# A mixture stage whose expert sum is split between VectorE, ScalarE and TensorE

## The reference

```python
logits = (h @ router_w.T + router_b).reshape(T, O, E)
probs = softmax(logits, axis=-1)
w, sel = top_k(probs, 2)
w = w / sum(w, axis=-1, keepdims=True)
c = zeros((T, E)).at[t_idx, sel].add(w)          # summed over all columns o
expert_out = einsum('th,eoh->teo', h, expert_w) + expert_b
final = einsum('te,teo->to', c, expert_out)
x = x + final
```

## Time and profile before

| | us |
|---|---|
| median of 3 runs (1189.95 to 1190.75) | 1190.35 |
| the profiled execution's own time | 1194.26 |
| its span | 1192.5 |
| mixture, first to last DVE instruction | 288.96 to 598.6 |
| busy in the span: PE / DVE / ACT / POOL | 1005.9 / 857.1 / 498.4 / 311.4 |
| busy from 288.9 to 598.7: PE / DVE / ACT / POOL | 239.26 / 291.58 / 165.23 / 113.89 |

### The profile page before, as it was taken

One profiled execution on the slowest core, in us unless ns is written; L12 is line 12 of the kernel. 1 busy time (PEld: TensorE's weight loads), 2 busy tenths in 40 slices (PEclk: granted clock), 3 DMA queues, 4 the chain that ended last, 5 costly groups with the idle time before them and its releaser, 6 DMA issues. The chain is left out here.

```text
span 1192.5 us, 19875 instructions
## 1 busy us (share of the span) xinstructions
PE 1005.9 (84%) x6885; PEld 588.9 (49%) x6960; DVE 857.1 (72%) x1556; ACT 498.4 (42%) x972; POOL 311.4 (26%) x337
## 2 busy tenths in 40 slices
PE   3698989888788798797487898898989799999997
PEld 1344545445444454353134474474657465556554
DVE  5677767643999899999967754746582776777766
ACT  2154444354464564646334313314230344444443
POOL 3243424531532524333320202203135400000000
PEclk9799989998899798898789898898897999999999
DMA  6622222101001000010000000001001000000000
GB/s 172 112 73 90 64 81 67 58 2 45 1 1 44 1 27 18 0 45 1 0 18 6 23 11 16 21 2 26 11 24 46 22 1 18 1 18 0 18 1 18
DMA packets 37088, 35.87 MB, mean 30 GB/s; under 512 B 8585, under 2 KB 33417, under 8 KB 37009
## 3 DMA queue, kind: packets, MB, share of 16 engines
q1 hardware_dynamic: 35728, 33.79, 9.8%
q10 hardware_dynamic: 1280, 1.05, 0.7%
HBM read 27.28 MB, written 6.29 MB: 28 GB/s over the span
## 5 line engine op out<-in xcount | busy, mean ns | idle before, releaser
L883 DVE TENSOR_REDUCE bm<-ps 128x4 f32<-128x512 f32 x160 | 102.1, 684 | 33.4 <-PE ps L603 31.7
L782 ACT ACTIVATE pt<-ps 128x1024 f32<-128x1024 f32 (+1 forms) x96 | 82.1, 882 | 72.5 <-PE ps L679 71.9
L1753 DVE TENSOR_TENSOR qk_lo<-ps,qk_hi 128x512 bf16<-128x512 f32 x80 | 54.9, 687 | 67.1 <-ACT qk_hi L1646 60.8
L2001 ACT ACTIVATE g<-ps 128x512 f32<-128x512 f32 x64 | 38.2, 597 | 134.1 <-PE ps L1948 107.4
L156 POOL TENSOR_TENSOR mag_w<-stage 128x512 f32<-128x512 fp8e4 x24 | 26.4, 1100 | 224.7 <-DVE stage L143 224.7
L2051 DVE SCALAR_TENSOR_TENSOR g<-g,ps 128x512 f32<-128x512 f32 x64 | 44.0, 688 | 54.5 <-ACT g L2001 54.2
L599 PE MATMUL ps<-ks,qs 96*128 96x512 bf16 (+3 forms) x256 | 66.7, 314 | 12.4 <-DMA ks<-scratch_k 7.7
L1646 ACT ACTIVATE qk_hi<-ps 128x512 bf16<-128x512 f32 x80 | 47.8, 599 | 69.4 <-PE ps L1515 69.4
L547 POOL TENSOR_SCALAR_AFFINE_SELECT pt<-pt 128x256 f32<-128x256 f32 (+1 forms) x96 | 47.2, 498 | 110.9 <-ACT pt L782 110.3
L1515 PE MATMUL ps<-wp_hi,oT_hi 128*128 128x256 bf16 x256 | 71.1, 278 | 5.0 <-DVE oT_lo L1746 5.0
L1964 PE MATMUL ps<-ew_hi,it_hi 128*128 128x256 bf16 x256 | 69.8, 273 | 6.1 <-DVE it_lo L2067 6.1
(11 more groups left out here) (272 smaller groups left out, 2840.9 us busy)
## 6 DMA issues: line engine op xcount, KB each, us to landing
qs<-scratch_q SPq DMA_DIRECT2D x64, 64.0 KB, 2.6
ks<-scratch_k SPq DMA_DIRECT2D x48, 64.0 KB, 2.6
q_next<-in_w_qkv SPq DMA_DIRECT2D x4, 768.0 KB, 4.4
X<-in_x SPq DMA_DIRECT2D x4, 512.0 KB, 7.0
w_next<-in_router_w SPq DMA_DIRECT2D x4, 512.0 KB, 3.7
w_next<-in_expert_w SPq DMA_DIRECT2D x4, 512.0 KB, 4.6
p_next<-in_w_proj SPq DMA_DIRECT2D x4, 512.0 KB, 5.4
out<-X SPq DMA_DIRECT2D x8, 256.0 KB, 2.3
```

The costliest lines, as they stand in the source:

```text
L782: act.activation(pt[kt][:, heads[0]:heads[-1] + 1, :], src, ACT.Exp).then_inc(s_exp, 1)
L883: ins = dve.tensor_reduce(bm[:, 2 * g + i // 5, 4 * (i % 5):4 * (i % 5) + 4], src.rearrange("p (k q) -> p k q", k=4), AX_X, ALU.max)
L1753: dve.tensor_tensor(qk_lo[:, k, h, :], bank(QK_BANK[m]), qk_hi[:, k, h, :], ALU.subtract).then_inc(s_qklo, 1)
```

## The change

`weigh` is cut in two. Experts 4 to 7 stay on DVE, as four multiply-adds. Experts 0 to 3 go to ACT, which writes psum * cw to a new tile `y` (`scaled_experts(n)`, behind `logits(n + 2)` and in front of `sigmoids(n + 1)`), and to PE, which sums the four parts of `y` with four fp32 matmuls against the identity into bank 4 (`scaled_sum(n - 1)`, behind `router(n + 2)`, or first in the iteration at t = 2). DVE adds that bank to X as its fifth instruction. PE fills the banks in the order 5, 6, 7, 4; bank 4 is free only when the whole `weigh(n - 1)` is done.

`two_greatest` is cut in two as well. Its first two instructions become `first_pairs`, done for tile n + 2. DVE's order in iteration n becomes: rest of `two_greatest(n + 1)`, `from_second(n + 1)`, statistics (t = 0), `first_pairs(n + 2)`, `masked(n + 1)`, `weigh(n)`. In the last two tiles the mask stays behind `weigh`. The tile `both` is gone; its place is taken by `n1`.

```diff
                 def experts(n, t):
-                    for u in range(NU):
-                        reach(pe, s_c, E * (n - 1) + 2 * (u + 1))
+                    for u in EXPERT_BANKS:                       # (1, 2, 3, 0)
+                        if u >= NY // 2:                         # NY = 4
+                            reach(pe, s_c, NX * (n - 1) + 2 * u + 2 - NY)   # NX = 5
+                        elif u == 0:
+                            reach(pe, s_c, NX * n)
+                def scaled_sum(n):
+                    pe.wait_ge(s_y, NY * n + NY)
+                    for e in range(NY):
+                        mm = pe.matmul(bank(4, D), ident[:, :], y[:, e, :], start=(e == 0), stop=(e == NY - 1),
+                                       skip_group_check=True)
+                    mm.then_inc(s_acc, 1)
                         if routed and t != 2:
                             router(routed[0], n + 2, routed[1])
+                        if not first or t:
+                            scaled_sum(n - 1)
                         experts(n, t)
+                def scaled_experts(n, t):
+                    act.wait_ge(s_cw, E * n + E)
+                    reach(act, s_acc, n)
+                    for u in EXPERT_BANKS:
+                        if u >= NY // 2:
+                            continue
+                        act.wait_ge(s_u, NU * n + EXPERT_BANKS.index(u) + 1)
+                        for e in (2 * u, 2 * u + 1):
+                            act.activation(y[:, e, :], bank(4 + u, D, D * (e % 2)), ACT.Copy,
+                                           scale=cw[t % 2][:, e:e + 1]).then_inc(s_y, 1)
+                        scaled_experts(n, t)
                         if after:
                             sigmoids(n + 1)
                 def weigh(b, n, t):
-                    for u in range(NU):
-                        dve.wait_ge(s_cw, E * n + 2 * u + 2)
-                        dve.wait_ge(s_u, NU * n + u + 1)
-                        for e in (0, 1):
-                            dve.scalar_tensor_tensor(x, bank(4 + u, D, D * e), c_t[:, 2 * u + e:2 * u + e + 1], x,
-                                                     ALU.mult, ALU.add).then_inc(s_c, 1)
-                            dve.wait_ge(s_c, E * n + 2 * u + e + 1)
+                    dve.wait_ge(s_cw, E * n + E)
+                    for i, e in enumerate(range(NY, E)):
+                        dve.wait_ge(s_u, NU * n + EXPERT_BANKS.index(e // 2) + 1)
+                        dve.scalar_tensor_tensor(x, bank(4 + e // 2, D, D * (e % 2)), c_t[:, e:e + 1], x,
+                                                 ALU.mult, ALU.add).then_inc(s_c, 1)
+                        dve.wait_ge(s_c, NX * n + i + 1)
+                    dve.wait_ge(s_acc, n + 1)
+                    dve.tensor_tensor(x, bank(4, D), x, ALU.add).then_inc(s_c, 1)
                         if after and not (first and t == 0):
-                            two_greatest(n + 1, after[1])
-                        weigh(b, n, t)
+                            two_greatest(n + 1)
+                        if after:
+                            from_second(n + 1, after[1])
                         if t == 0 and not last:
                             statistics(b + 1)
+                        if routed:
+                            first_pairs(n + 2, routed[1])
+                        if after and routed:
+                            masked(n + 1)
+                        weigh(b, n, t)
+                        if after and not routed:
+                            masked(n + 1)
                         if last and t == 1:
                             next_statistics()
-                        if after:
-                            from_second(n + 1, after[1])
-                            masked(n + 1)
```

More of the change, by code:

```diff
@@ L166 @@
 NU = EO // BANK
+NY = 4
+NX = E - NY + 1
+EXPERT_BANKS = (1, 2, 3, 0)
 STEP = 1.5 * 2.0 ** -22
@@ L969, in layer0_mixture @@
         h2, a2, c2 = (st.sb(n, [P, 2, D], F32) for n in ("h2", "a2", "c2"))
-        m1, n1, c1, m2, both, mid = (st.sb(n, [P, D], F32) for n in ("m1", "n1", "c1", "m2", "both", "mid"))
+        m1, n1, c1, m2, mid = (st.sb(n, [P, D], F32) for n in ("m1", "n1", "c1", "m2", "mid"))
         cw = [st.sb(f"cw{n}", [P, E], F32) for n in range(2)]
+        y = st.sb("y", [P, NY, D], F32)
         load_next, s_next, const = st.sem("load_next1"), st.sem("next1"), st.sem("const1")
@@ L982, in layer0_mixture @@
         s_abs, s_pert = st.sem("magnitudes"), st.sem("ties_broken")
+        s_y, s_acc = st.sem("experts_scaled"), st.sem("scaled_summed")
         stats2, mv2, rstd2 = (glob[n] for n in ("stats2", "mv2", "rstd2"))
@@ L1139, in _ @@
                 all_batches(pe, batch)
+                scaled_sum(4 * B - 1)
             @block.scalar
@@ L1258, in step, with first_pairs @@
                         dve.wait_ge(self.sem, self.start + self.done)
-                def two_greatest(n, t):
+                def first_pairs(n, t):
                     L = lg[t % 2]
@@ L1267, in two_greatest @@
                     do.step(dve.tensor_tensor(s4[:, :, :], L[:, 0:4, :], L[:, 4:8, :], ALU.min))
+                def two_greatest(n):
+                    do = Steps(s_top, TOP * n)
+                    do.done = 2
                     do.free(dve.tensor_tensor(h2[:, :, :], h4[:, 0:2, :], h4[:, 2:4, :], ALU.max))
@@ L1275, in two_greatest @@
                     do.step(dve.tensor_tensor(m2[:, :], n1[:, :], c1[:, :], ALU.max))
-                    do.step(dve.tensor_tensor(both[:, :], m1[:, :], m2[:, :], ALU.add))
+                    do.step(dve.tensor_tensor(n1[:, :], m1[:, :], m2[:, :], ALU.add))
                     if not isinstance(n, int) or n:
                         dve.wait_ge(s_mid, n)
-                    do.free(dve.tensor_scalar(mid[:, :], both[:, :], 0.5, None, ALU.mult))
+                    do.free(dve.tensor_scalar(mid[:, :], n1[:, :], 0.5, None, ALU.mult))
                     assert do.done == TOP
@@ L1311, in next_statistics @@
                 def next_statistics():
-                    dve.wait_ge(s_c, E * (4 * B - 3))
+                    dve.wait_ge(s_c, NX * (4 * B - 3))
                     for b in range(B):
@@ L1332, in next_low @@
                                           ALU.subtract)
-                two_greatest(0, 0)
+                first_pairs(0, 0)
+                two_greatest(0)
                 from_second(0, 0)
-                two_greatest(1, 1)
+                first_pairs(1, 1)
+                two_greatest(1)
                 masked(0)
                 def batch(b, first, last):
-                    for t, n, after, _ in tiles(b, last):
+                    for t, n, after, routed in tiles(b, last):
                         if t == 1 and not last:
```

## The result

The changed kernel takes **1230.17 us** (median of 4 runs, 1228.63 to 1232.07) against 1190.55 for the kernel before (4 runs, 1189.95 to 1192.47) on the same chip. The ratio is 1.0318, 95% interval 1.0290 to 1.0345: about 40 us slower. The forecast was 1218, its own range 1210 to 1232. The profiled execution took 1230.55, its span is 1228.8, 36.3 longer than before's. The two gaps differ because before's profiled execution (1194.26) lay 3.7 us above the median of its runs and after's only 0.4.

A forecast was written before the change was run, and what follows sets the result against it. The prediction took mutual exclusion between POOL's `wt` and DVE's two-SBUF-input instructions as the bound in every tile. Terms 1.6 + 5.5 + 14.4 + 7.5 - 1 gave +28.0 on 1190.35: 1218 us, own range 1210 to 1232, overall 1207 to 1234.

The forecast's parts named there:

- two batches of the loop: Mixture loop: tiles t = 0 to 3 lose 0.7, 0.9, 3.2 and 2.4 us, +7.2 a batch, +14.4 for two.
- tiles 13 to 15: Last batch: 61.4 us instead of 53.88, +7.5, with 19.1 each for tiles 13 and 14 and 23.2 for tile 15.
- The block (1): DVE between `mid` and mask: `far` and two comparisons exclude POOL's `wt`, together 8.99 us in every tile.
- The sums (2): DVE behind the mask: four sums plus a fifth instruction of 0.5, 2.9 us in the loop, 2.55 outside.
- ACT's lateness at t = 2 (3): Tile t = 2: late router, scalings and sigmoids end 0.4 to 1.8 us behind the comparisons; 0.8 taken, tile 21.1.
- The last root (5): Tile 15: POOL's root between statistics and `normalised` loses its cover and costs 1.7 us.
- The tail (6): Behind the last mask: the last sum ends 9.1 us after that mask's start instead of 10.3, so -1.
- PE's cost (7): PE in the mixture: 64 added fp32 matmuls, about 1.5 us a tile, cost zero; bounds 0 to +2 a batch.
- The range for unknowns: Whole change: ACT's lateness, fifth instruction, register waits, last root and PE's clock together give +20 to +42 us.
- no exclusion: First rival: `wt` runs beside `far` and comparisons, tile 17.25 us, 1192 us, no change; 6 in 100.
- DVE's count decides: Second rival: three fewer DVE instructions save 1.9 us a tile, 16 times, -30, so 1160 us; 5 in 100.
- PE becomes the bound: Rival: PE idles, its clock falls, tiles close through PE: +45 to +60, 1235 to 1250 us; 7 in 100.

The follow-up runs named there:

- e1: Kernel before with only DVE's order of the changed kernel, all eight sums staying on DVE behind the mask: 1248.26 us, ratio 1.0469.
- e2: Changed kernel with DVE's order of before, five sum instructions beside POOL's `wt`, scalings and scaled sum issued one step earlier: 1199.08 us, ratio 1.0058.
- e3: Changed kernel with `wt` made by DVE between `mid` and `far` instead of by POOL: 1202.89 us, ratio 1.0094.
- e5: Changed kernel with POOL's `wt` subtraction replaced by a memset of the same tile, so POOL only writes: 1172.34 us (one run).
- e10: e9 with one more move on PE: at t = 3 the scaled sum stands ahead of the router: 1218.54 us, ratio 1.0215.
- e9: Changed kernel; at t = 2 `x_low` ahead of the sums, router and ties ahead of the experts, scalings behind the sigmoids: 1229.48 us, ratio 1.0317.
- e6: e2 with four of `wt`'s eight experts made by DVE ahead of the sums, the rest by POOL beside them: 1186.19 us, ratio 0.9956.

## Why the prediction was right

The block of `far`, `wt` and two comparisons is within 0.6 us of the forecast in every tile but the three at t = 2, where ACT's late copies hide it, and the last, which has no comparisons. e1, e2, e3 and e5 each show it from another side. By the terms of the forecast, with what they measured from mask to mask:

| term | forecast | measured |
|---|---|---|
| tile 1 of batch 0 | +1.6 | +1.8 |
| tiles 2 to 4 | +5.5 | +7.0 |
| two batches of the loop | +14.4 | +17.0 |
| tiles 13 to 15 | +7.5 | +7.3 |
| tail | -1 | +1.3 |
| sum | +28.0 | +34.4 |

Another 1.25 us lie ahead of the first mask and 0.7 elsewhere in the span. Of the 11.8 us between the forecast and the median, 8.3 are in the span. The other 3.5 are the step from the span to the median: the forecast took off the 3.9 us by which before's profiled execution lay above its median, and after's lay only 0.4 above.

- **The block (1).** 8.99 us was the forecast for `far` and both comparisons; it is 8.95 in the last tile of batch 0 (382.75 to 391.70) and 8.96 in the loop (467.41 to 476.37). Right. At t = 1 it is 9.38, since POOL's small instruction stretches the second comparison (1.69 for 1.21).
- **The sums (2).** The fifth instruction was a bound between 0 and 0.52; it takes 0.42, in all 16 tiles, and four sums and addition take 2.4 us outside the loop and 2.5 in it, against 2.55 and 2.9. This, and not the block, makes t = 0 (18.9 for 19.45) and t = 3 (21.85 for 22.25) a little shorter. That t = 1 takes just the forecast 20.75 is luck: 0.4 less in the sums, 0.4 more in the block.
- **ACT's lateness at t = 2 (3).** The mis-sized term. "It starts 1.5 to 3 us behind `x_low`" was said of the router; it starts 4.6 behind (437.33 to 441.91). I had counted PE's work behind the sums at the full clock, 2.4 GHz; a lower one stood only among the unknowns. PE idles 5.6 us first, and its next 13 matmuls stand 0.43 us apart where they stand 0.215 apart at the full clock: 2.8 us. The trace of before could have told me: there too PE comes back at 0.50 after 5.19 us without work (window of the matmuls behind it):

```profile
464.60:469.00 4.40, 4.40 (x15) 2.42 (x15) 4.20 (x9) 3.25 (x7) 1.20 (x2) 0.50 0.00 0
```

  Forecast 0.8 late, measured 2.9 (23.2 for 20.3). Over three batches t = 2 is 5.7 above the forecast; with the tail's 2.3, and 1.6 less in the other terms, these are the 6.4 us that the sum is short. e10 takes the lateness out. That its median is the predicted time is chance: the mixture there is 24.8 us longer than before, not 28.
- **The last root (5).** 1.7 us was forecast, 1.68 measured; tiles 13 to 15 61.16 for 61.4. Right.
- **The tail (6).** Forecast 9.1 behind the last mask's start, measured 11.6. Nearly all of it is the last scaled sum, 1.5 in the forecast, 3.78 in the trace. DVE waits for it, and PE's row shows why:

```profile
633.78 0.42 DVE L1342 TENSOR_TENSOR X<-ps,X 128x256 f32<-128x256 f32 x1 [2.92 <-PE ps L1126]
...
629.90 3.78 PE L1126 MATMUL ps<-y,ident 128*128 128x256 f32 x8 [8.03 <-ACT y L1212]
```

- **PE's cost (7).** Four matmuls show as eight records: 1.9 us at the full clock, up to 3.8 at 0.50, so 1.5 was low. It cost nothing in 15 tiles of 16, as said. But the term looked for PE's price in its work. It is in its place: three batches at t = 2, and the tail.

Of the rivals, *no exclusion* and *DVE's count decides* are out by e3 and e5 and by e2. *PE becomes the bound* was right in one tile of four, t = 2, where the tile closes through PE, and wrong in its size: +6 and not +17 to +32 over the forecast. Its clock did not fall further: a batch of the loop has 0.90 in the mean, where before had 0.89. PE waits 4.6, 1.2, 5.6 and 0 us for the sums at t = 0 to 3, and its clock falls to 0.50 behind the first and the third of these waits, and for some 2 us at the scaled sum of t = 2; before had two such stretches in a batch as well, from 408.5 to 416.5 and from 464.6 to 469.0. In the first rival, 74.8 us a batch is 0.5 more than its own terms give (four times 17.25, and 5.3 of extras); nothing rests on it. The range for unknowns, +20 to +42, held the +36.3 of the span. In the whole mixture DVE's busy sum rose from 291.58 to 303.31 us, as forecast.

Not settled: of e2's 7 us over before, 1.65 are placed in the mixture by the profiles (batch 0 and the tail lose more than the loop gains), and the rest isn't explained; and e9 and e10 move three queues at once; which of the moves would do alone was not tried.

## What to carry to other kernels

Before taking work from an engine, look at what the neighbouring engine does in the same microseconds: here the instructions that were moved and cut were the long ones of every tile that could run beside a reading POOL instruction. When a step is moved ahead in one queue, move all that hangs on it (router, ties, copies, scaled sum), and read the interval of the next tile too, or the gain is given back there. When one engine shuts another out, cut its instruction to the length of the work that may run beside it: with POOL's part cut to the length of the sums, the kernel became 0.5% faster than before.

## What the hardware showed that was not expected

- Time in which DVE is shut out by POOL is counted as busy: the same comparison (`h<-lg`) averages 1.77 us before and 5.55 us after, with no idle time in front of it. Compare an instruction's mean with its shortest before believing an engine's share.
- Whoever is taken up later waits out the other, and they take turns: `wt` waits for `far`, then the comparison for `wt`, although DVE could have gone on directly.
- A 128 x 2048 write on POOL (1.81 us) runs beside DVE's two-input read undisturbed. The subtraction of 128 x 1024 shows 3.24 us in e6, of which 0.99 is the wait for DVE's half (until 449.18): 2.25 is just half of the 4.5 of 128 x 2048.
- A 256-column fp32 matmul is two records of 0.24 us spacing at the full clock and 0.47 at a granted clock of 0.50 (eight records in 1.89 us in e9, in 3.78 us in the tail).
